# Attention scores as single float16 products over 64-row strips that hold both halves of q and k

## The reference, cut to what matters

```python
h = tok(x)                                  # patches @ W_lin.T + b, class token in front
qkv = layernorm(h) @ qkv_weight.T           # 12 heads of 16 features
q = layer_norm(q) * 16 ** -0.5              # over the 16 features of a head
k = layer_norm(k)
attn = softmax(einsum('bhnd,bhmd->bhnm', q, k))
out = einsum('bhnm,bhmd->bhnd', attn, v)
h = h + out @ proj_weight.T
h = h + mixture_of_experts(layernorm(h))    # phase B, untouched
```

## Time and profile before

| | |
|---|---|
| median of the runs | 1763.53 us |
| the profiled execution's own time | 1764.9 us |
| its span in the profile | 1763.0 us |
| TensorE busy | 1695.0 us, 96% |
| VectorE busy | 1290.8 us, 73% |
| ScalarE busy | 984.6 us, 56% |
| GpSimd busy | 336.7 us, 19% |
| phase A ends, about | 1009 us from the span's start |

### The profile page before, as it was taken

One profiled execution on the slowest core, in us unless ns is written; L12 is line 12 of the kernel. 1 busy time (PEld: TensorE's weight loads), 2 busy tenths in 40 slices (PEclk: granted clock), 3 DMA queues, 4 the chain that ended last, 5 costly groups with the idle time before them and its releaser, 6 DMA issues. The chain is left out here.

```text
span 1763.0 us, 45476 instructions
## 1 busy us (share of the span) xinstructions
PE 1695.0 (96%) x17682; PEld 1180.2 (67%) x17682; DVE 1290.8 (73%) x3660; ACT 984.6 (56%) x2088; POOL 336.7 (19%) x402
## 2 busy tenths in 40 slices
PE   4999999999999999999999599999999999999998
PEld 4777777777777777777777345555555555555555
DVE  4677776666666666666666278888888888888887
ACT  2666666666666666666666354454545454545453
POOL 1000000000000000000000033434343434344433
PEclk8999999999999999999999799999999999999999
DMA  7233333333333333333320101010101010101000
GB/s 230 66 74 74 74 75 74 74 74 70 70 72 74 73 73 73 74 75 74 74 54 12 42 10 37 20 37 19 37 20 37 19 37 19 37 19 37 16 19 16
DMA packets 40866, 95.26 MB, mean 54 GB/s; under 512 B 4491, under 2 KB 17454, under 8 KB 40526
## 3 DMA queue, kind: packets, MB, share of 16 engines
q1 hardware_dynamic: 31438, 72.89, 13.2%
q0 software_dynamic: 9216, 19.47, 7.3%
HBM read 92.44 MB, written 19.37 MB: 63 GB/s over the span
## 5 line engine op out<-in xcount | busy, mean ns | idle before, releaser
L1309 POOL TENSOR_TENSOR in_lo<-inner,in_hi 128x512 f16<-128x512 f32 (+1 forms) x225 | 257.7, 1145 | 433.7 <-ACT act L1096 433.7
L575 ACT ACTIVATE prob<-ps_sc 99x792 f32<-99x792 f32 x384 | 310.7, 827 | 53.1 <-PE ps_sc L390 53.1
L1242 DVE SCALAR_TENSOR_TENSOR acc<-ps_y,comb,acc 128x192 f32<-128x192 f32 (+1 forms) x700 | 241.9, 407 | 0.3 <-PE ps_y L1038 0.3
L1104 ACT ACTIVATE in_hi<-inner 128x512 f16<-128x512 f32 (+1 forms) x225 | 140.3, 623 | 181.3 <-DVE inner L1224 181.3
L1096 ACT ACTIVATE act<-ps_h 128x512 f32<-128x512 f32 (+1 forms) x225 | 131.8, 586 | 189.7 <-PE ps_h L1022 189.7
L1224 DVE SCALAR_TENSOR_TENSOR inner<-ps_h,act 128x512 f32<-128x512 f32 (+1 forms) x225 | 153.7, 683 | 103.4 <-ACT act L1096 99.8
L1036 PE MATMUL ps_y<-w_hi,in_hi 128*128 128x192 f16 (+1 forms) x900 | 224.1, 249 | 4.1 <-DVE acc L1242 1.9
L1038 PE MATMUL ps_y<-w_hi,in_lo 128*128 128x192 f16 (+1 forms) x900 | 221.6, 246 | 0.0
L1037 PE MATMUL ps_y<-w_lo,in_hi 128*128 128x192 f16 (+1 forms) x900 | 221.5, 246 | 0.0
L331 PE MATMUL ps_hid<-lin_hi,x_hi 128*99 128x192 f16 x768 | 192.7, 251 | 21.3 <-DVE x_lo L685 10.6
L844 POOL DMA_DIRECT2D x_hi<-xp x64 | 34.0, 532 | 869.5 <-PE ps_hid L333 868.7
(11 more groups left out here) (154 smaller groups left out, 3670.5 us busy)
## 6 DMA issues: line engine op xcount, KB each, us to landing
xin<-xp SPq DMA_DIRECT2D x64, 594.0 KB, 4.3
x_hi<-xp POOLq DMA_DIRECT2D x64, 297.0 KB, 4.0
hidden_dram<-h SPq DMA_DIRECT2D x64, 147.0 KB
hin<-hidden_dram SPq DMA_DIRECT2D x24, 384.0 KB, 3.1
out<-acc SPq DMA_DIRECT2D x24, 384.0 KB, 2.3
w_f<-w SPq DMA_DIRECT2D x1, 2304.0 KB, 8.9
hidden_dram<-h SPq DMA_DIRECT2D x64, 0.8 KB
w_f<-w SPq DMA_DIRECT2D x1, 864.0 KB, 10.8
```

The source lines that it names most:

```text
L575: act.activation(prob[quad][:, places].rearrange("p h m s -> p h (m s)"), ps_sc[0:TR, places, 0:2 * SLOTS], ACT.Exp, scale=D ** -0.5 / (SQ ...
L1242: last = dve.scalar_tensor_tensor(out=acc[p][0:R, t, :], in0=ps_y[half_no][0:R, u * C:(u + 1) * C], scalar=comb[p][0:R, t, e:e + 1], in1=b ...
L1309: pool.tensor_tensor(in_lo[b][:, 0:N], inner[b][:, 0:N], in_hi[b][:, 0:N], ALU.subtract).then_inc(inlo_done, 1)
```

## The change

q and k are normalised as before, now into a dense `qk_norm` (16 values a head). Two new steps follow. `qk_high` on ScalarE rounds all 384 values to float16 and writes each twice. `qk_low` on VectorE subtracts the rounded values from `qk_norm` and writes the remainders as float16. In `qk_strips` a head has 64 values: for q remainder, leading, leading, zero, and for k leading, leading, remainder, zero. One float16 product over these 64 rows gives all three terms of the split product. The transposes are now six float16 ones of 128 columns (two heads each) for q and six for k, and the copies out of PSUM are 128 by 594 float16. `scores` runs eight float16 matmuls of 64 rows a quad, two heads beside one another.

```diff
-            qk_norm = [sa(f"qk_norm{t}", [TR, 2 * HEADS, QB]) for t in range(2)]
-            qT = [sa(f"qT{p}", [128, QUADS, SLOTS]) for p in range(2)]
-            kT = [sa(f"kT{p}", [128, QUADS, SLOTS]) for p in range(2)]
+            qk_norm = [sa(f"qk_norm{t}", [TR, 2 * HEADS, D]) for t in range(2)]
+            qk_strips = [sa(f"qk_strips{t}", [TR, 2, HEADS * HS + 3 * KSHIFT], F16) for t in range(2)]
+            id16 = sa("id16", [128, 128], F16)
+            qT = [sa(f"qT{p}", [128, CHUNKS, SLOTS], F16) for p in range(2)]
+            kT = [sa(f"kT{p}", [128, CHUNKS, SLOTS], F16) for p in range(2)]
...
             def transpose_qk(n, t, w):
                 if w == 0:
-                    pe.wait_ge(qknorm_done, n.times(2, t + 1))
+                    if n.c == 0 and t == 0:
+                        pe.wait_ge(id16_set, 1)
+                    pe.wait_ge(qklo_done, n.times(2, t + 1))
...
-                for b in range(QUADS):
-                    last = pe.transpose(qkT_ps[:, b, :], part[:, b, :], id32[0:TR, 0:TR])
+                for b in range(CHUNKS):
+                    last = pe.transpose(qkT_ps[:, b, :], flat[t][:, w * KFIRST + b * 128:w * KFIRST + b * 128 + 128],
+                                        id16[0:TR, 0:TR])
...
-                        rows = slice(QB * place, QB * place + QB)
-                        last = pe.matmul(sc[:, place, m, :], kT[p][rows, quad, m * TR:(m + 1) * TR],
-                                         qT[p][rows, quad, :], start=True, stop=True)
+                        rows = slice(HS * (place % 2), HS * (place % 2) + HS)
+                        chunk = 2 * quad + place // 2
+                        last = pe.matmul(sc[:, place, m, :], kT[p][rows, chunk, m * TR:(m + 1) * TR],
+                                         qT[p][rows, chunk, :], start=True, stop=True)
...
+            def qk_high(n, t):          # ScalarE
+                act.wait_ge(qknorm_done, n.times(2, t + 1))
+                if reached(n.times(4, 2 * t - 2)):
+                    act.wait_ge(qkT_done, n.times(4, 2 * t - 2))
+                act.activation(high_twice[t], qk_norm[t][:].unsqueeze(2).broadcast_to([TR, 2 * HEADS, 2, D]), ACT.Copy).then_inc(qkhi_done, 1)
...
                     exponent(n4, 2, 1)
+                if n3.active():
+                    qk_high(n3, 1)
+                if n4.active():
                     oT_copy(n4, 1)
...
                     square(n2, 1)
+                    qk_high(n2, 0)
                     qk_rstds(n2, 1)
...
+            def qk_low(n, t):           # VectorE
+                dve.wait_ge(qkhi_done, n.times(2, t + 1))
+                dve.tensor_tensor(low_once[t], qk_norm[t][:].rearrange("p (b h) d -> p b h d", b=2), high_once[t],
+                                  ALU.subtract).then_inc(qklo_done, 1)
...
                 if n3.active():
+                    qk_low(n3, 1)
                     kT_copy(n3, 0)
...
                 if n5.active():
                     residual(n5)
                 if n2.active():
+                    qk_low(n2, 0)
                     qk_normalise(n2, 1)
...
+            act.wait_ge(consts_a_loaded, 16 * len(consts_a))
+            act.activation(id16[:], id32[:], ACT.Copy).then_inc(id16_set, 1)
...
             for t in range(2):
-                pool.memset(qk_norm[t][:], 0.0)
+                pool.memset(qk_strips[t][:], 0.0)
```

More of the change, by code:

```diff
@@ L37 @@
 QUADS = HEADS // QUAD
-QB = 32
+HS = 64
+CHUNKS = HEADS // 2
+KSHIFT = D
 VB = 32
@@ L194, in phase_a @@
      h, stats, meanvar, h_rstd, h_lnvar, xnorm, xT_hi, xT_lo, qk_sq, qk_var, qk_lnvar, qk_rstd,
-     qk_norm, qT, kT, v, prob, oT, o_rden, o_norm, onT_hi, onT_lo, h2) = (
+     qk_norm, qk_strips, id16, qT, kT, v, prob, oT, o_rden, o_norm, onT_hi, onT_lo, h2) = (
         bufs[n] for n in (
@@ L198, in phase_a @@
             "h stats meanvar h_rstd h_lnvar xnorm xT_hi xT_lo qk_sq qk_var qk_lnvar qk_rstd "
-            "qk_norm qT kT v prob oT o_rden o_norm onT_hi onT_lo h2").split())
+            "qk_norm qk_strips id16 qT kT v prob oT o_rden o_norm onT_hi onT_lo h2").split())
     with ExitStack() as ctx:
@@ L212, in phase_a @@
         qk_ps = ps_qk[0:TR, 0:2 * C].rearrange("p (h d) -> p h d", d=D)
-        qkT_ps = ps_mix[:, 0:QUADS * TR].rearrange("p (b s) -> p b s", s=TR)
+        qkT_ps = ps_mix[:, 0:CHUNKS * (TR + 1) // 2].bitcast(F16).rearrange("p (b s) -> p b s", s=TR + 1)[:, :, 0:TR]
+        KFIRST = HEADS * HS + KSHIFT
+        flat = [x[:].rearrange("p b e -> p (b e)") for x in qk_strips]
+        strips = [x[:, D:D + 2 * HEADS * HS].rearrange("p (h e) -> p h e", e=HS) for x in flat]
+        high_twice = [x[:, :, 0:2 * D].rearrange("p h (two d) -> p h two d", two=2) for x in strips]
+        high_once = [x[:, :, 0:D].rearrange("p (b h) d -> p b h d", b=2) for x in strips]
+        low_once = [x[:, :, 0:HEADS * HS].rearrange("p b (h e) -> p b h e", e=HS)[:, :, :, 0:D] for x in qk_strips]
         o_feat = ps_mix[:, 0:2 * SLOTS].rearrange("p (k s) -> p k s", k=2)
@@ L245, in phase_a @@
             sem("xnorm_done"), sem("xTlo_done"), sem("qkvar_done"), sem("qknorm_done"))
+        qkhi_done, qklo_done, id16_set = sem("qkhi_done"), sem("qklo_done"), sem("id16_set")
         rden_done, onorm_done, onTlo_done, h2_done = (
@@ L369, in transpose_qk @@
                 if w == 0:
-                    pe.wait_ge(qknorm_done, n.times(2, t + 1))
+                    if n.c == 0 and t == 0:
+                        pe.wait_ge(id16_set, 1)
+                    pe.wait_ge(qklo_done, n.times(2, t + 1))
                 if reached(n.times(4, 2 * t + w)):
                     pe.wait_ge(qkT_out, n.times(4, 2 * t + w))
-                part = qk_norm[t][:, w * HEADS:(w + 1) * HEADS, :].rearrange("p (b h) e -> p b (h e)", h=QUAD)
-                for b in range(QUADS):
-                    last = pe.transpose(qkT_ps[:, b, :], part[:, b, :], id32[0:TR, 0:TR])
+                for b in range(CHUNKS):
+                    last = pe.transpose(qkT_ps[:, b, :], flat[t][:, w * KFIRST + b * 128:w * KFIRST + b * 128 + 128],
+                                        id16[0:TR, 0:TR])
                 last.then_inc(qkT_done, 1)
@@ L731, in qk_normalise @@
                 dve.wait_ge(qkrstd_done, n.times(2, t + 1))
-                if reached(n.times(4, 2 * t - 2)):
-                    dve.wait_ge(qkT_done, n.times(4, 2 * t - 2))
-                dve.tensor_tensor(qk_norm[t][:, :, 0:D], qk_ps,
+                if reached(n.times(2, t - 1)):
+                    dve.wait_ge(qklo_done, n.times(2, t - 1))
+                dve.tensor_tensor(qk_norm[t][:], qk_ps,
                                   qk_rstd[:].unsqueeze(2).broadcast_to([TR, 2 * HEADS, D]),
                                   ALU.mult).then_inc(qknorm_done, 1)
+            def qk_low(n, t):
+                dve.wait_ge(qkhi_done, n.times(2, t + 1))
+                dve.tensor_tensor(low_once[t], qk_norm[t][:].rearrange("p (b h) d -> p b h d", b=2), high_once[t],
+                                  ALU.subtract).then_inc(qklo_done, 1)
             def kT_copy(n, t):
```

## The result

The changed kernel takes 1776.95 us (median of 4 runs, 1775.62 to 1777.93), against 1763.04 us for the one before (median of 4). The ratio is 1.008, 95% interval 1.0065 to 1.0095. The forecast was slower, 1789 us with a range of 1768 to 1816. The direction and the mechanism held. The size was 13.9 us in place of 25.

A forecast was written before the change was run, and what follows sets the result against it. It took a closed loop through TensorE, ScalarE and VectorE as the bound: 60 steps x 0.39 = 23.4 us, +2.6 for steps with pieces, about -1 for fill and drain, together +25, so 1789 us, range 1768 to 1816.

The forecast's parts named there:

- What bounds the kernel: Phase A: TensorE, 96% busy, doesn't set the 14.82 us period alone; VectorE is late at the step's end.
- the loop: Phase A step: TensorE's transposes, ScalarE's copy of q and VectorE's list to o_norm close a cycle of 14.82 us.
- Scores, transposes: TensorE: float16 scores save about 0.35 us a quad, 1.05 a step; six float16 transposes take what three float32 took.
- all three savings: The three score quads of a step: each quad's saving of about 0.35 us falls into waits.
- The copies: Out of PSUM: ScalarE's copy of q grows from 0.42 to 0.66 us; VectorE's copy of k stays at 0.47.
- the rival of the slow copy: VectorE's copy of k runs at one element a cycle, 20 us more: 1809 us; chance 18%.
- qk_high and qk_low: Rounding: ScalarE's two and VectorE's first cost nothing; VectorE's second, 0.55 us long, stands on the loop.
- The loop after: End of a phase A step: o_by_token(n4, 1) starts 0.39 us later, giving a period of 15.21 us.
- The steps with pieces: 13 steps with pieces of expert weights: ScalarE 0.62 us later, the loop feels about 0.2, +2.6 us in all.
- TensorE alone: Phase A: TensorE alone sets the period, which falls towards 13.54 us: 1687 us, or 1725 for half; chance 8%.
- Slow transposes: TensorE: float16 transposes stay at 0.083 us each, 0.2 a group on the loop, +36: 1825 us; chance 7%.
- The clock: TensorE's idle pieces let some steps be granted 1.2 GHz, a tenth of them adding 72: 1860 us; chance 3%.

The follow-up runs named there:

- E1: Changed kernel with every score product issued twice (16 float16 matmuls a quad in place of 8): 1777.45 us, ratio 1.0092, period 15.05 us.
- E3: Changed kernel with ScalarE copying only 3 of the 6 blocks of q out of PSUM, the others zero: 1754.59 us, ratio 0.9957, period 14.69 us.
- E7: Kernel before the change plus qk_high and qk_low at their four places, writing to tiles that nothing reads: 1769.74 us, ratio 1.0045, period 14.94 us.
- E2: Changed kernel with both qk_low instructions moved from VectorE to GpSimd: 1770.53 us, ratio 1.0053, period 14.93 us.
- E4: Changed kernel with the first transposes of q going to the free bank of ps_qk in place of ps_mix: 1742.26 us, ratio 0.9894.
- E5: Changed kernel with the edits of E4 and E2 together: 1742.58 us, ratio 0.9879, period 14.46 us.
- E8: Changed kernel with E4's edit, residual before qk_variance on VectorE and exponent before qk_rstds on ScalarE: 1729.33 us, ratio 0.9804.

## Why the prediction was right, and where its size was off

*What bounds the kernel.* Right. The row with a wait for o_norm in 54 of 54 steps was the sign that TensorE, though 96% busy, wasn't alone. E1 shows it for the kernel after: a whole microsecond more of TensorE's work a step doesn't change the period. The sign that would have refuted the loop, idle time of VectorE between residual and o_norm, is absent (500.61 to 502.75).

*Scores, transposes.* Right in size: a quad's records last 0.55 us (495.54) in place of 0.93, and a group of six transposes 0.44 in place of 0.42. That all three savings fall into waits needs a limit. With the long copy of q they do (E1). With the short one 0.25 us a step come through, 0.21 of them where the last quad stands (E3 against E7). The forecast had TensorE's idle time at about 1.6 us a step; it is 1.2, since the period grew by less.

*The copies.* Right. The copy of k stayed at 473 ns with twice the elements, so the rival of the slow copy (767 ns, +20 us) fell. The Trainium skill (VectorE: DVE Perf Modes, "Why PSUM operands drop a tier") allows a copy out of PSUM two packed 16-bit values a cycle and one float32 value. The trace agrees: 473 ns for 594 float16 elements after, 467 for 297 float32 elements before. ScalarE has no such gain, 672 ns in place of 420. Its longer copy is the largest cost of the change, 0.36 us a step by E3.

*qk_high and qk_low.* Right in place. The first of each and the second qk_high lie in idle time. The second qk_low is on the loop: 0.12 us a step by E7 and by E2.

*The loop after.* The step that was mis-sized. The forecast had o_by_token at +0.39, measured is +0.23. The difference of 0.16 comes from these terms. From qk_normalise to the start of o_norm I carried over 0.82 us (511.95 to 512.77); after, it is 0.72 (501.54 to 502.26). Before, the reciprocal between them had started 0.56 behind qk_normalise, when o_by_token's result was there. After, that result was early enough, and the reciprocal followed in 0.46, as other VectorE instructions do. That is 0.10. (In E2 o_by_token is the later one again, and the 0.56 is back.) The list from the copy of k to qk_normalise was shorter by 0.09 (11.03 in place of 11.12), in pieces of 0.01 to 0.03. From the transposes' weight loads to ScalarE's copy are 0.48 and not 0.53. In the other direction, the copy took 0.68 and o_by_token's loads started 0.11 behind its end, not 0.05: together 0.08 back.

*The steps with pieces.* Wrong. I added 0.2 us in 13 steps for ScalarE's late start. They measure 15.05, as all others. In ten of them the change costs 0.11 to 0.12 and not 0.59: a delay that bound before (14.94 against 14.82) is hidden now behind the longer loop. The other three had no such delay before, and cost 0.23, though ScalarE's instruction is the longest there (0.67 us, against 0.62 in the nine and 0.21 in the last). So how late ScalarE starts isn't what the delay went by; what it was, no run shows. The sum had 60 x 0.39 + 2.6 = 26 us for the steps, where the 56 steps between the two issues took 11.9. The steps with pieces make up 10 x 0.48 + 3 x 0.36 = 5.9 of what was too much, and the others 47 x 0.16 = 7.5. The small terms were right: -1 us for the first and last steps, where the first steps measure -0.9, and nothing for the memset.

*A wait that I missed.* o_by_token(n4, 0) waits 0.5 us for residual. The forecast had 0.9 for o_norm in one piece; measured are 0.51 for residual and 0.34 for o_norm. In the changed kernel this did no harm, since the reciprocal that reads o_by_token's result followed qk_normalise in 0.46. In E2 it did, by 0.10. That it held back E4 and E5 too is likely from their rows, but E8 took it away together with the wait for the exponential, so its own share is not shown.

*The rivals.* TensorE alone: refuted by E1 (15.05 in place of 16.05). Slow transposes: refuted, 0.44 us a group. The clock: the granted clock is 1.00 in 200 to 900 us before and after, at its level of 2.4 GHz, with TensorE busy 643 us of the 700 in place of 692. The Trainium skill says that transposes don't count as activity of TensorE in the same way (TensorE: Matmul & The Clock Gate, "Part 4: PE-mode transpose"). This would have spoken for a fall; no run here shows one.

## What to carry to other kernels

An engine that is 96% busy but waits once in every step at the same place isn't the bound by itself: follow that wait around until the loop closes, and price a change by what it adds to the loop. Work that a change takes off TensorE comes back as waits if it lengthens the hand-overs through PSUM; here the cure was not less work but a free bank, which was worth 0.09 us a step before the change and 0.58 after it. A gap of a fixed length is no constant of the code: before carrying a gap from one profile to the next, ask which of two conditions ended it.

## What was not expected of the hardware

The forecast had both lengths right, but no row of the kernel before showed a float16 read of PSUM. A float16 transpose written to PSUM and copied by VectorE costs hardly more for twice the elements (473 against 467 ns), while ScalarE pays for every element (672 against 420). When an engine is to copy float16 out of PSUM, the choice of engine is thus worth 0.2 us in 594 elements.
